# One more batch's shared feed-forward inside the attention turns, fewer pieces beside the experts, and two transposes of the expert loop exchanged

## The reference

```
x = x + xattn(layernorm(x), ctx)              # 16 heads of 128, 8 key/value heads, softmax over 256 keys
h = layernorm(x)
topk_idx, topk_w = gate(h)                    # 4 of 32 experts for each row, 2 of 4 groups
buf[e, slot] = h[row], at most CAP = 128 rows for each expert, first come first served
ob  = (silu(buf @ w1) * (buf @ w3)) @ w2      # F = 256, for each expert
out = sum over the 4 choices of topk_w * ob[expert, slot]
shared = (silu(h @ shared_gate) * (h @ shared_up)) @ shared_down    # FS = 512
x = x + out + shared
```

## Time and profile before

| | us |
|---|---|
| median of three runs | 1654.64 |
| the profiled execution's own time | 1655.04 |
| its span, first to last instruction | 1653.3 |
| PE busy | 1611.9 (97%) |
| DVE busy | 1213.4 (73%) |
| ACT busy | 821.8 (50%) |
| POOL busy | 807.3 (49%) |

### The profile page before, as it was taken

One profiled execution on the slowest core, in us unless ns is written; L12 is line 12 of the kernel. 1 busy time (PEld: TensorE's weight loads), 2 busy tenths in 40 slices (PEclk: granted clock), 3 DMA queues, 4 the chain that ended last, 5 costly groups with the idle time before them and its releaser, 6 DMA issues. The chain is left out here.

```text
span 1653.3 us, 34814 instructions
## 1 busy us (share of the span) xinstructions
PE 1611.9 (97%) x12194; PEld 1153.0 (70%) x12194; DVE 1213.4 (73%) x3510; ACT 821.8 (50%) x2034; POOL 807.3 (49%) x1130
## 2 busy tenths in 40 slices
PE   7999999999999999999999999999999999999994
PEld 4767777777777686777777777777776777656552
DVE  6887776767777676777678778787877765777783
ACT  5764443534344444444354554544454433677782
POOL 2444554536363645455455463646455357343443
PEclk9999999999999999999999999999999999999997
DMA  7754343434333433434344545445453487599984
GB/s 231 186 150 84 78 84 78 94 69 97 70 86 71 99 67 75 83 80 83 78 110 88 104 99 109 104 96 110 90 117 65 103 284 227 162 283 266 304 247 64
DMA packets 395054, 205.69 MB, mean 124 GB/s; under 512 B 347889, under 2 KB 356081, under 8 KB 394881
## 3 DMA queue, kind: packets, MB, share of 16 engines
q1 hardware_dynamic: 380720, 181.32, 45.5%
q0 software_dynamic: 13600, 21.10, 6.5%
q10 hardware_dynamic: 560, 1.05, 0.2%
HBM read 87.67 MB, written 32.41 MB: 73 GB/s over the span
## 5 line engine op out<-in xcount | busy, mean ns | idle before, releaser
L961 ACT ACTIVATE arena<-arena,neg_max 128x256 f32<-128x256 f32 x512 | 253.7, 496 | 378.1 <-DVE neg_max L1268 378.1
L698 POOL TENSOR_SCALAR arena<-arena,prob_scale 128x256 f16<-128x256 f32 x384 | 183.9, 494 | 457.0 <-DVE prob_scale L1277 441.1
L1619 PE MATMUL ps_query<-xn_both,arena 128*128 128x256 f16 x1024 | 280.3, 274 | 1.3 <-DMA xn_both<-xn_half 1.3
L1621 PE MATMUL ps_query<-xn_both,arena 128*128 128x256 f16 x1024 | 280.3, 274 | 0.0
L1620 PE MATMUL ps_query<-xn_both,arena 128*128 128x256 f16 x1024 | 280.3, 274 | 0.0
L1268 DVE CUSTOM_DVE_ANT_0 arena<-ps_score,mask_add 128x256 f32<-128x256 f32 x512 | 186.7, 420 | 121.9 <-PE ps_score L1621 121.9
L1283 DVE SCALAR_TENSOR_TENSOR arena<-arena,prob_scale 128x256 f16<-128x256 f32 x384 | 233.3, 655 | 7.3 <-POOL arena L698 7.3
L1619 PE MATMUL ps_out<-arena,o_t 128*128 128x512 f16 x512 | 194.1, 379 | 3.2 <-DVE o_t L1288 3.2
L1620 PE MATMUL ps_out<-arena,o_t 128*128 128x512 f16 x512 | 194.0, 379 | 0.0
L1621 PE MATMUL ps_out<-arena,o_t 128*128 128x512 f16 x512 | 194.0, 379 | 0.0
L753 POOL DMA_INDIRECT slot_table<-entry,slot_at x128 | 133.4, 1043 | 48.2 <-issue 33.3
(11 more groups left out here) (325 smaller groups left out, 4045.3 us busy)
## 6 DMA issues: line engine op xcount, KB each, us to landing
arena<-w SPq DMA_DIRECT2D x96, 512.0 KB, 6.6
x_in<-x SPq DMA_DIRECT2D x15, 512.0 KB, 3.6
xn_rows<-xn_half SPq DMA_DIRECT2D x15, 512.0 KB, 3.2
out_rows_dram<-x SPq DMA_DIRECT2D x30, 256.0 KB, 2.4
ctx_in<-ctx_t SPq DMA_DIRECT2D x16, 256.0 KB, 3.1
weight_in<-wq SPq DMA_DIRECT2D x8, 512.0 KB, 5.1
weight_in<-wo SPq DMA_DIRECT2D x8, 512.0 KB, 4.6
arena<-arena SPq DMA_TRANSPOSE x256
```

Source lines behind the costliest of these rows:

```text
L698: pool.tensor_scalar(p_rows[:, c, 0, :], probs[:, c, :], prob_scale[:, c:c + 1], 1.0, ALU.mult, ALU.mult).then_inc(norm_hi, 1)
L961: act.activation(probs[:, c, :], probs[:, c, :], ACT.Exp, bias=neg_max[:, c:c + 1], scale=-1.0, accum_out=prob_sum[:, c:c + 1]).then_inc(e ...
L1619: pe.matmul(dst, a.hi, b.hi, start=start and n == 0, stop=False)
L1621: m = pe.matmul(dst, a.lo, b.hi, start=False, stop=stop and n == len(pairs) - 1)
```

## The change

Four edits:

1. DEFER is 9 and LATE has seven batches: the shared feed-forward of batch 8 is done in the turns of batch 9, like those of batches 0 to 7, with its sum made in SBUF. KEPT is 3, so one batch fewer goes through DRAM.
2. PIECES has 42 entries; EARLY stays 24, so 18 run beside experts, and BESIDE leaves out experts 7 and 15: they stand beside 0 to 6, 8 to 14 and 16 to 19. Experts 7, 15 and 20 to 31 have none.
3. `add_in` becomes {8: s3 and s4, 20: s5 and s6}.
4. On PE `expert_hidden(e)` stands ahead of `expert_rows(e + 2)`.

```diff
-DEFER = 8
-LATE = (8, 9, 14, 15, 10, 11, 12, 13)
-KEPT = len(LATE) - 4
+DEFER = 9
+LATE = (9, 10, 14, 15, 11, 12, 13)
...
-    if EARLY + len(BESIDE) < len(PIECES):
+    if _e % 8 != 7 and EARLY + len(BESIDE) < len(PIECES):
         BESIDE[_e] = EARLY + len(BESIDE)
...
-        x2t_kept = nc.dram_tensor("x2t_kept", (KEPT, P, 2 * KD * T), F16, kind="Internal").ap()
+        x2t_kept = nc.dram_tensor("x2t_kept", (3, P, 2 * KD * T), F16, kind="Internal").ap()
...
-        add_in = {max(e + e % 2, 4): ns for ns in ((3,), (4, 5), (6, 7)) for e, k in BESIDE.items()
-                  if PIECES[k] == ("d", ns[-1], TB - 1)}
+        add_in = {e + e % 2: (n - 1, n) for n in (4, 6) for e, k in BESIDE.items() if PIECES[k] == ("d", n, TB - 1)}
...
-                sp.wait_ge(out_x2t, 16 * KEPT)
+                sp.wait_ge(out_x2t, 48)
...
-                if AHEAD - 1 <= e < AHEAD - 1 + KEPT:
+                if AHEAD - 1 <= e < AHEAD + 2:
                     load_x2t(e - AHEAD + 5)
...
+                if e < E:
+                    expert_hidden(e)
                 if e + 2 < E:
                     expert_rows(e + 2)
-                if e < E:
-                    expert_hidden(e)
```

More of the change, by code:

```diff
@@ L288, in build @@
         out_x2t = signal("out_x2t")
-        in_x2t = [signal(f"in_x2t{n}") for n in range(KEPT)]
+        in_x2t = [signal(f"in_x2t{n}") for n in range(3)]
         added_first, added = signal("added_first"), signal("added")
```

## The result

| | before | changed |
|---|---|---|
| median | 1652.08 us (6 runs, 1647.55 to 1655.04) | 1660.13 us (6 runs, 1658.25 to 1667.75) |
| ratio to before | | 1.0062, 95% interval 1.0043 to 1.0082 |
| profiled execution, span | 1653.3 us | 1656.4 us |

The changed kernel is slower by 0.62%, some 10 us (7 to 14 by the interval); the two medians lie 8.0 us apart. The two profiled executions differ by 3.1 us only: the one of before lost 2.9 us at its very start (first head copy at 35.36 us against 32.45 us, with a granted clock of 0.91 in the first 40 us against 1.00), and the changed kernel's profile is one of its quickest executions. So stages are compared from the tanh of expert 0 on, and the verdicts rest on the timed runs.

What follows compares the result with a forecast made beforehand. The prediction took POOL's serial chain of output additions to set the end: its last odd addition moves from 1641.06 to 1645.5 us, so 1654.64 + 4.4 = 1659.0 us, with a range of 1651 to 1666.

Steps and rivals of the forecast that it cites:

- Part 1: Attention turns: six pieces moved into batch 9's turns, where PE is the bound, cost 15.43 us that nothing hides.
- Part 2: Expert stage: six experts lose their piece and save 2.2 us each; tanh of expert 20 at 1569.8 us.
- Part 3: POOL's chain of additions: last shared group at expert 20; last pair's odd addition starts at 1645.5, 4.4 us later.
- Loaded gaps: POOL's chain: while weights load, an even addition to the next group takes 9.2 us, measured between 7.19 and 10.85.
- The wait behind the group: POOL's chain: pair (18, 19) waits 13.0 us behind four shared additions, with weights loading.
- the upper bound: POOL's chain with every gap at its upper end, the group 14 us: last start at 1652, 11 us later.
- The start of that sum: POOL's chain: even addition of pair (16, 17) taken at about 1569.1 us, just ahead of expert 20's tanh.
- Part 4: PE's expert stage: hidden transposes first cost 0.2 us in each of 12 bare experts, 2.4 us, nothing at the end.
- Rival 3: Expert stage, 12%: queues overload behind expert 20, late gathers or weights stall PE 5 to 8 us; 1666 us.
- Rival 1: End of kernel, 15%: additions meet fewer weights, the last output sets the end; -5 us, some 1649.5.
- Rival 2: POOL's chain, 28%: shorter gaps cancel the loss, chain 0 to 3 us late; within 0.2%, 1655 to 1658 us.
- the upper rival: The slower case, starved experts behind expert 20, given 12% and 1666 us; the same as Rival 3.

Runs made afterwards that it cites:

- e1: Kernel before with one edit, the hidden transposes put ahead of the rows transposes; ratio to before 0.9995.
- e6: Changed kernel with the gathers for experts 28 to 31 one place earlier in POOL's list; ratio to before 1.0063.
- e2: Changed kernel with the transposes back in the old order, rows ahead of hidden; ratio to before 1.0045.
- e4: Changed kernel with the last shared group left out, shared parts of batches 12 and 13 computed but not added; ratio to before 1.0001.
- e8: Changed kernel with weight loads of experts 26 to 31 cut to 64 of 1024 columns in each third; ratio to before 0.9983.
- e9: Changed kernel with only POOL's last shared group moved, from expert 20 to expert 24; ratio to before 1.0053.
- e11: Kernel before with its 24 pieces beside experts 2 to 25 and not 0 to 23; ratio to before 0.9976.
- e7: Changed kernel with its 18 pieces beside experts 6 to 23, shared groups at experts 14 and 24; ratio to before 1.0017.
- e10: Kernel before with weight loads of experts 26 to 31 cut to 64 of 1024 columns in each third; ratio to before 0.9967.

## Why the prediction was right, step by step

The direction, the bound and the range came out right; the size did not. 4.4 us were forecast, and the ratio gives 10 us (7 to 14). The time of 1659.0 us is close to the measured 1660.13 only because the kernel before ran at 1652.08 us in the compared runs and not at the 1654.64 that the sum started from.

- **Part 1, the attention turns: right.** 15.43 us were forecast and batch 9 shows 89.45 us. The expert stage began only 10.7 us later in the profiled pair, because of the 2.9 us at the start of the one before and 1.9 us less in batch 14 (74.31 us before, 72.40 changed). Neither comes from the change: e1, with the pieces of the kernel before, takes 71.90 us for batch 14, and e6, with those of the changed one, has its first head copy at 35.38 us. Over all profiles the tanh of expert 0 is 13.9 us later with the changed pieces (mean of eight) than without (mean of six).
- **Part 2: a little too dear.** A lone bare expert saves 7.70 - 5.03 = 2.7 us, not 2.2. With the early start this put the tanh of expert 20 at 1563.94 instead of 1569.8.
- **Part 3, the chain: the mechanism was right, one term mis-sized.** From the even addition of pair (16, 17) to the odd one of (30, 31), 76.4 us were forecast and 1644.67 - 1564.10 = 80.6 measured. Loaded gaps of 9.2 us: 9.76 and 9.71. The wait behind the group, 13.0: 15.74. The gap ahead of pair (22, 23), 7.2: 5.5. Cycles at the end, 7.79: 8.0. The wait of 15.74 lies beyond even the 14 us of the upper bound, and e2 and e6 show 17.1 and 17.7. The forecast of 1645.5 for the last odd addition met 1644.67 only since the early start (5.0 us) and the longer chain (4.2 us) cancel; that is luck. Without it the loss is 4.4 + 4.2 = 8.6 us, which the interval of the timed runs holds.
- **The start of that sum was an assumption that often fails.** The sum lets the even addition of pair (16, 17) keep pace with PE, 1.2 us ahead of a tanh, as (20, 21) does in the kernel before. It was 0.2 us behind in the profile of the changed kernel, and 7.4 us behind in e2, e4, e6 and e8. With the pieces of the kernel before the chain has until expert 24 to make up such a lag: in e1 it is 6.3 us behind at expert 20 and 0.2 us at 24.
- **Part 4: right in that it costs nothing, the number by luck.** Bare experts take 11.0 us for two (10.8 before), PE waits 0.2 us ahead of ps_head, and e1 shows no cost in time. The last output at 1636.4 (forecast 1637.5) is a cancellation again: the expert stage began 4.7 us earlier than forecast, and the step of 10.67 us gave it back. That DVE and ACT were close to full was misread: they were busy 34.23 and 31.21 of 44 us.
- **Rival 3 came in part.** I gave it 12% as a case of its own; it came on top. PE waited 2.8 us in this profile, 9.2 in e2, 5.6 in e6. That is one of the signs by which the prediction called itself wrong, so its picture of PE behind expert 24 was wrong; its bound was not, as e9 shows. The prediction considered the gathers for 29 to 31. The late ones were those for 27 (e2, e6) and 28 (the changed kernel). The gather directly behind the shared group shares its wait: 13.7 us from issue to PE's start in e2, 14.2 in e6. Executions of the changed kernel spread from 1656.4 to 1667.8 us, but the kernel before spreads as far on one chip (1655.4 to 1667.1), so the spread says nothing of these waits.
- **Rival 1 failed:** its point of decision was a loaded gap under 7 us; the two single gaps that the sum took at 9.2 were 9.8 and 9.7 us, and e8 gave it 6.5 us only by taking the weights away. **Rival 2** (it cancels) falls by the ratio's interval.

The rule that each DMA engine takes the queues in turn, packet by packet (the Trainium skill, "DMA: Bandwidth & Descriptors", "Queues, rings and completion order") was used to hold the upper rival down. In the changed kernel's profile the gaps of single additions agree (9.2 before, 9.7 in the full stretch); in e2 they are 10.3 to 11.9 us. The group of four doesn't fit that use of it: 15.7 us with all engines full, 10.1 us with light loads.

What stays open: why the chain lags by 7 us at expert 20 in some executions and not in others; whether the kernel before would gain as much as e4 without its last group; and where e11 gains. That PE's waits add something to the 10 us in the slowest executions isn't excluded, but no run shows it.

## What to carry to other kernels

Filler work taken away from an engine can have a price elsewhere: bare experts asked for their weights sooner one after another, the DMA engines were full with these and the output additions, and the serial chain of additions was what ended last. When filler work is moved, ask what the emptied places will demand of the queues: here the same 18 pieces cost 10 us with the bare experts among the last loads and 3 us with them where nothing was loading (e7). A serial chain of transfers is priced by gaps measured at the same load of the queues, and a group of transfers, with whatever queues behind it, by more than a single one. And a wait on the busiest engine is worth nothing by itself: e9 had none and was as slow, since another chain ended last.

## What the runs showed of the hardware

- The gap from an accumulating 256 KB addition to the next one waiting for it: 5.9 us with idle queues, 6.5 with light loads (e8), 7.2 to 10.9 beside weight loads in the kernel before and up to 11.9 in e2. Behind four such additions: 10.1 and 11.0 us with light loads (e8, e10), 11.5 and 13.0 in the kernel before, 15.7, 17.1 and 17.7 with the DMA engines full (changed, e2, e6).
- The DMA engines moved 340 GB/s in the full stretch of the changed kernel (share 1.05), and 282 in a stretch of the kernel before whose share was 0.95 already. So the share of busy time did not tell how much more they could move.
- Behind a wait of 2.8 us PE's matmuls of 512 columns took 0.63 us and not 0.38, at a granted clock of 0.57 in 1602 to 1606 us.
